# Expert stages: who releases GpSimd's scatters, and how far ahead the sync engine loads rows

## The reference

```python
x = x + attention_block(layernorm(x))   # 16 heads, learned relative bias, MLP
x = x + ffn(layernorm(x))               # 8 experts, the best 2 for each row
x = x + recurrence(layernorm(x))        # gated scan along the sequence
x = x + ffn(layernorm(x))               # the same experts once more
```

```python
probs = softmax(xf @ router_w.T)           # keep the top 2, renormalise
g = einsum('nd,edf->nef', xf, gate_w) + gate_b
u = einsum('nd,edf->nef', xf, up_w) + up_b
h = silu(g) * u
expert_out = einsum('nef,efd->ned', h, down_w) + down_b
y = einsum('ne,ned->nd', probs, expert_out)
```

## Time and profile before

| | before |
|---|---|
| time, median of 3 runs | 1426.32 us |
| lowest and highest | 1423.66, 1427.49 us |
| span of the profiled execution | 1524.2 us |
| PE, DVE, ACT, POOL busy | 80%, 75%, 63%, 65% |
| POOL's scatters (L1842), both stages | 272, 263.8 us busy |

### The profile page before, as it was taken

The page is one execution under the profiler, slowest core; times in us unless marked ns, Lnnn a source line. Parts: engine busy times, 40 slices in busy tenths (PEclk is TensorE's granted clock), DMA queues, the critical chain, the costliest instruction groups (busy, mean ns, idle before and its releaser), DMA issues. The chain is left out here.

```text
span 1524.2 us, 38116 instructions
## 1 busy us (share of the span) xinstructions
PE 1216.6 (80%) x11689; PEld 1017.3 (67%) x11689; DVE 1144.1 (75%) x3833; ACT 967.7 (63%) x2078; POOL 991.9 (65%) x1131
## 2 busy tenths in 40 slices
PE   5889999999999999973788888577787449888850
PEld 3667777777777777753788888455566348788850
DVE  5489999999999999965566665488888546666638
ACT  3588888888888888851555544277777435455420
POOL 4346688888888888777355665237777835666530
PEclk9699999999999999995799997588878669999955
DMA  7211111111111111123222222112222122222228
GB/s 199 86 46 46 48 60 60 60 60 60 59 60 60 60 60 60 39 93 83 73 86 86 81 85 68 49 49 83 73 83 69 45 68 84 86 84 84 77 83 277
DMA packets 99443, 117.19 MB, mean 77 GB/s; under 512 B 17784, under 2 KB 79792, under 8 KB 99248
## 3 DMA queue, kind: packets, MB, share of 16 engines
q1 hardware_dynamic: 70560, 73.57, 16.3%
q0 software_dynamic: 16896, 35.16, 6.8%
q10 hardware_dynamic: 11792, 6.05, 1.4%
HBM read 47.56 MB, written 41.51 MB: 58 GB/s over the span
## 5 line engine op out<-in xcount | busy, mean ns | idle before, releaser
L1153 DVE TENSOR_TENSOR ebuf<-score_banks,region 128x768 f32<-128x768 f32 x256 | 243.6, 951 | 18.8 <-PE score_banks L862 13.1
L1402 ACT ACTIVATE region<-ebuf 128x768 f32<-128x768 f32 x256 | 215.9, 860 | 23.0 <-DVE ebuf L1153 23.0
L1380 ACT CAST copied<-max_banks 128x768 bf16<-128x768 f32 x251 | 201.9, 804 | 15.1 <-PE max_banks L850 12.5
L1842 POOL DMA_INDIRECT choice_rows<-second_yo,second_xg x136 | 133.1, 979 | 112.7 <-PE second_by L1880 69.3
L1842 POOL DMA_INDIRECT choice_rows<-first_yo,first_xg x136 | 130.7, 961 | 114.0 <-PE first_by L1880 65.9
L1694 POOL DMA_INDIRECT expert_rows<-d_rows,a_d_index x112 | 129.4, 1155 | 27.9 <-issue 17.2
L1918 ACT ACTIVATE second_silu<-second_bgu,second_biases 128x256 f32<-128x256 f32 (+1 forms) x144 | 61.0, 466 | 114.3 <-PE second_bgu L1871 66.7
L1918 ACT ACTIVATE first_silu<-first_bgu,first_biases 128x256 f32<-128x256 f32 (+1 forms) x144 | 61.9, 462 | 111.8 <-issue 83.6
L1954 DVE SCALAR_TENSOR_TENSOR second_hT<-second_bgu,second_biases,second_silu 128x256 f32<-128x256 f32 (+1 forms) x144 | 62.1, 464 | 70.3 <-ACT second_silu L1918 37.6
L905 PE MATMUL bankO<-region,vaug 128*32 128x256 f32 (+1 forms) x2048 | 111.1, 334 | 1.9 <-ACT region L1402 1.9
L853 PE MATMUL max_banks<-region_r 32*128 32x256 f32 x502 | 98.3, 388 | 11.9 <-DVE ebuf L1153 7.4
(11 more groups left out here) (369 smaller groups left out, 4531.6 us busy)
## 6 DMA issues: line engine op xcount, KB each, us to landing
region_r<-region_r SPq DMA_DIRECT2D x192, 128.0 KB
first_xg<-expert_rows SPq DMA_DIRECT2D x64, 132.0 KB
second_xg<-expert_rows SPq DMA_DIRECT2D x64, 132.0 KB
z_rows<-choice_rows SPq DMA_DIRECT2D x32, 256.0 KB
c_rows<-choice_rows SPq DMA_DIRECT2D x16, 512.0 KB
out<-xres ACTq DMA_DIRECT2D x16, 256.0 KB
choice_rows<-first_yo,first_xg POOLq DMA_INDIRECT x136
choice_rows<-second_yo,second_xg POOLq DMA_INDIRECT x136
```

The source lines that it names most:

```text
L1153: nc.vector.tensor_tensor(ebuf[:, half_of_ebuf(c, j), :, :], score_banks[:, :, 0:BK], bias32[:, plain(j), :], ALU.add).then_inc(scores_fre ...
L1380: nc.scalar.copy(copied[:, 2 * j:2 * j + 2, :], banks_of_max(c, j)[:, :, 0:BK]).then_inc(maxed_free, 1)
L1402: nc.scalar.activation(p32[:, j % 4, :, :], ebuf[:, half_of_ebuf(c, j), :, :], ACT.Exp).then_inc(exped, 1)
L1842: pool.indirect_dma_start(choice_dram, bass.IndirectOffsetOnAxis(ap=xg[:, i % G, t, E:E + 1].bitcast(I32), axis=0), yo[:, i % 4, t, :], No ...
```

## The change

Both expert stages come from the same function, so both change. GpSimd no longer waits for `y_full` and `y_done`, but for one new semaphore, `rows_go`. SyncE raises it: for each turn it waits for VectorE's sum (`y_done`), raises `rows_go` by one, and then loads the rows six turns ahead. It loads six turns before the loop, where it loaded up to eight turns ahead before. The wait for `xT_full` is dropped, the one for `stored` stays. Buffers and arithmetic are the same.

```diff
-    G = 8
+    G, AHEAD = 8, 6
...
+        ..., b_ready, wh_ready, wl_ready, rows_go = (
...
                 for i in range(ST):
-                    pool.wait_ge(y_full, min(i + 2, ST))
-                    pool.wait_ge(y_done, i + 1)
+                    pool.wait_ge(rows_go, i + 1)
                     for t in range(T(i)):
                         pool.indirect_dma_start(
...
             def _(sp):
-                for i in range(ST):
-
+                def load(i):
                     if i >= G:
-                        sp.wait_ge(xT_full, i - G + 1)
                         sp.wait_ge(stored[i % 4], stored_to(i - G))
                     first = sp.value_load(...)
                     sp.dma_start(xg[:, i % G, ...], slots_dram[...]).then_inc(arrived[i % G], 16)
+
+                for i in range(AHEAD):
+                    load(i)
+                for i in range(ST):
+                    sp.wait_ge(y_done, i + 1)
+                    sp.sem_inc(rows_go, 1)
+                    if i + AHEAD < ST:
+                        load(i + AHEAD)
                 for q in range(4):
                     sp.wait_ge(stored[q], stored_to(max(range(q, ST, 4))))
```

More of the change, by code:

```diff
@@ L1820, in run_dispatched @@
         stored = [sem(f"rows_stored{i}") for i in range(4)]
-        xT_full, hi_done, lo_done, gu_full, silu_done, hid_done, y_full, y_done, b_ready, wh_ready, wl_ready = (
+        xT_full, hi_done, lo_done, gu_full, silu_done, hid_done, y_full, y_done, b_ready, wh_ready, wl_ready, rows_go = (
             sem("xT_full"), sem("hi_done"), sem("lo_done"), sem("gu_full"), sem("silu_done"), sem("hid_done"),
-            sem("y_full"), sem("y_done"), sem("biases_ready"), sem("upper_weights_ready"), sem("lower_weights_ready"))
+            sem("y_full"), sem("y_done"), sem("biases_ready"), sem("upper_weights_ready"), sem("lower_weights_ready"), sem("rows_go"))
         def stored_to(i):
```

## The result

| | before | changed |
|---|---|---|
| time, median | 1425.08 us (5 runs) | 1414.97 us (5 runs) |
| lowest and highest | 1423.64, 1427.49 us | 1411.92, 1420.54 us |
| ratio, with its 95% interval | | 0.9919 [0.9893, 0.9945] |
| PE, DVE, ACT, POOL busy | 80%, 75%, 63%, 65% (the execution of the earlier trace rows) | 82%, 81%, 70%, 70% |

The changed kernel is 0.81% faster by the ratio, some 11.5 us of 1425 (1 - 0.9919); the two medians differ by 10.1 us. The median of 1414.97 is outside the forecast's own range of 1422 to 1428 and 0.6 us from rival A's 1415.6.

A forecast was written before the change was run, and what follows sets the result against it. At 2.54 us a turn PE was taken to bound the expert stages, POOL's 2.52 close behind. Only the stage ends counted, -1.4 us from a median of 1426.3, giving 1424.9 us (own range 1422 to 1428, whole range 1413 to 1437).

The forecast's parts named there:

- rival A: Row buffers did bind PE in timed runs; earlier scatters free them: -10.7 us, 1415.6 us, chance 0.25.
- The pace in whole turns: Expert stages: profile stays at 3.2 us a turn; timed runs estimated at PE's 2.54 us.
- The ring of eight buffers: Load of turn i + 8 waits for scatter i: needs 19.0 to 21.5 of 20.3 us; gain 0, bounds 0 to 19.
- How far a scatter moves: Scatter waits for its sum, not the next down product: starts one turn earlier, 2.5 to 3.2 us.
- The end of a stage: Last two scatters of each stage: scatter 71 starts 0.7 us earlier, -1.4 us in two stages.
- The hand-over: Sum's end to scatter through SP: 0.4 us, 0.1 of it SP; bounds 0.15 and 1.5; costs nothing in whole turns.
- The loads six turns ahead: Load i waits for sum i - 6: 5.1 us left for 3.4 needed; cost 0, up to 2 us a stage.
- rival C: Loads, each hanging on a sum six turns back, come late and stall PE: 14 us, 1439 us, chance 0.10.
- Rival B: Scatters meet DVE's weight copies of `wlo` and POOL becomes the bound: +10 on the forecast, 1434.9 us, chance 0.15.
- Rival D: POOL is never idle in timed runs, so scatters start where they did, tail gains nothing: 1426.3 us, chance 0.08.

The follow-up runs named there:

- e5: Kernel before with twelve row buffers instead of eight, scatters still as late as before; 1416.06 us, ratio 0.993.
- e1: Kernel before, unedited, profiled once more; 1429.09 us, ratio 1.0013.
- e11: Kernel before, unedited, profiled another time; 1429.84 us.
- e3: Kernel before, with POOL's wait for the next down product dropped only in the last eight turns of a stage; 1424.55 us, ratio 0.9987.
- e7: Changed kernel without the relay: POOL waits for the sum itself, SP still paces its loads by it; 1414.79 us, ratio 0.9915.
- e2: Kernel before, with POOL's scatters waiting for the sum alone, SP and its loads as before; 1416.0 us, ratio 0.9929.
- e10: Changed kernel with loads five turns ahead, not six; 1475.32 us, ratio 1.0343.
- e8: Changed kernel with loads seven turns ahead, not six; 1463.42 us, ratio 1.0258.
- e6: Kernel before, with eight added one-tile buffers for the last eight loads, which then wait for no scatter; 1416.99 us, ratio 0.9939.
- e4: Changed kernel, with SP also waiting for the next down product before it releases the scatter; 1432.43 us, ratio 1.0043.
- e9: Kernel before with twelve row buffers and scatters that wait for the sum alone, no relay; 1414.35 us, ratio 0.9921.

## Why the prediction was right in part and wrong in its likeliest case

The stated range of 1413 to 1437 us holds the measured 1414.97, but the case called likeliest, 1424.9 and no measurable change, was not what happened. Rival A, the ring of buffers, did happen, with the right sum for a partly wrong reason.

- **The pace in whole turns: right in the estimate, wrong as a forecast of the profile.** The estimate that the timed runs go at PE's 2.54 us held (2.54 to 2.57 in all profiles of before and after). "The pace of 3.2 us in whole turns should stay" was wrong: 3.2 was a property of that one execution. Why it ran so is open; none of the later ones did.
- **The ring of eight buffers: the step that failed.** The prediction set the way round the ring, 19.0 to 21.5 us, against 20.3, eight whole turns, and said "I take a gain of 0". The measured way round was 20.9 us, inside those bounds, with a landing that was late; with the usual one it is about 19. What it was set against was wrong where it matters: the last loads serve one-tile turns, and eight turns from 62 on last 17.9 us (e5). With 17.9 on the other side of the comparison all of 19.0 to 21.5 is late, by 1.1 to 3.6 us; e1 showed 2.33, e11 2.05. Only the whole turns had been looked at. For the whole turns the step was nearly right: 0.8 us less in the first stage, 0.3 more in the second.
- **How far a scatter moves: over-sized.** "One turn earlier, 2.5 to 3.2 us" was 0.8 us in whole turns. The sum ends 1.0 us after its own product, so the next product is only 1.5 us away, and POOL itself had no room for more than 0.8. At turn 62 it was 1.5 us, of which 0.7 are the held scatter of turn 56, which no term of the prediction had.
- **What follows from a stall was missing.** The bound priced a wait at its own length. In the second stage the stall of 2.3 us was followed by 4.2 us of slower matmuls at the lower clock, twice what the wait cost. This term stood nowhere in the sum.
- **The end of a stage: right.** 0.7 us was expected, 0.8 measured in both stages; e3, which has this and little else, is 0.13% faster than before, a difference within its interval.
- **The hand-over: over-sized, without effect.** 0.4 us from the sum to the scatter was taken, 0.31 measured, of which SP is 0.03 (e7) and not 0.1. It lies inside the bounds of 0.15 and 1.5.
- **The loads six turns ahead: right at 0.** e7 and e2 agree within their intervals, and PE does not wait for rows in the whole turns of the changed kernel (745 to 890 us), so rival C did not happen. The estimate of 1.7 us of room fits: one turn less, 2.54 us, does not fit into it and is 3.4% slower (e10). One turn more is 2.6% slower, by the wait for landings (e8).
- **Rival B: seen, too small.** Scatters of over 1.0 us were 17 and 12 of 136 in the changed kernel, 3 and 3 in e1, and each of these 35 overlaps a copy of `wlo` on DVE, while the longest scatter of the changed kernel that overlaps none took 0.969 us. So the earlier scatters do meet the copies more often. But the median is 0.959 us in the changed kernel and 0.961 and 0.962 in e1, and the pace of PE did not change. The rule from "SBUF — State Buffer", section "SBUF: two separate sides" of the Trainium skill, by which the loser blocks for the whole instruction, would make many scatters 0.43 us longer. The trace does not agree: 97 scatters of the changed kernel have a whole copy of `wlo` within their time, at a median of 0.959 us, and the longest of all was 1.167 us.
- **Rival A's price was right by luck.** It took two thirds of the 14 us that PE had waited before transposes all along the stages in the unusual execution. The measured gain has the same size but sits in the last eight turns, mostly of the second stage.
- **Rival D** is excluded by the ratio's interval. But its ground was half right: POOL had no room for more than 0.8 us of the 1.5 that the change set free.
- **A reading that was off, without effect.** The prediction says that POOL waits 0.9 to 1.0 us of each turn of 3.19 us. 3.19 - 2.52 is 0.67; the 0.94 to 1.02 us of idle time in the earlier trace rows contain the 0.30 us that follow every scatter. No term of the sum hangs on it.

**Late landings.** From the end of a pair's second scatter to the moment when SP's wait for it is over it is mostly 1.3 to 2.2 us. For turn 62 of the second stage it was 3.44 us in e1, 3.35 in e11 and 3.49 in e3, so this late landing came back in three executions and is no accident of one. The traces' DMA packets show a companion: a packet of 16 KB in the queue that the profile's page calls instruction (q8), in e1 from 1362.48 to 1363.56 us. Of the 32 packets of turn 62's second scatter 31 had begun by 1362.5; the last one began at 1363.54. In the profiles of e1, e2, e3, e6, e7 and e11 42 of the 48 landings over 2.4 us, and all 16 over 3.0, had such a packet in flight, of the other 665 only 130. That these packets delay the scatters is argued from this, no run moved them. In e3 one ran from 1351.90 to 1353.56 us, while the rows of turn 69 were on their way. With e1's usual landing the way round the ring would have been about 19 us, still over 17.9, so the late one makes the stall longer but, by this estimate, does not make it alone. Without the 0.7 us of the held scatter as well it would be about 18, and the ring would just close.

**The clock.** That PE's stall came just before the drop is shown in e1 (2.33 us) and e11 (2.05), and in e3, where waits of 1.75 and 0.53 us came before it. e5 and e6 changed only the buffers and had neither stall nor drop, nor had e2 and the changed kernel. But no length of wait can be read from this: in e3's first stage PE waited 0.96 us at 903.4 us and the clock stayed at 1.00, and in e4's second stage it fell after a wait of 0.76 us (at 1363.3 us).

What one typical timed run gains in the last parts is not shown directly, as the two profiled executions of before (timed at 1432.9 and 1429.8 us) lie above their jobs' medians of 1425.8 and 1427.9, and those of the changed kernel (1411.9 and 1412.9) below its 1415.0. That most timed runs have the drop is likely: their granted clock over the whole run is 0.915 to 0.917 on average for the kernel before in the three jobs, 0.9145 in e3, and 0.921 to 0.924 in the changed kernel, e2, e5, e6, e7 and e9.

## What to carry to other kernels

Compare a ring of buffers with the time of the turns it really spans, the shortest ones at the end of a loop included, not with the steady pace. A consumer that is as fast as the producer in the steady pace falls behind when turns shorten, and then each needless wait ahead of it counts. A ring that just closes has no room for a landing that is 1 to 2 us late. Price a stall of PE with the slower clock that can follow it, and ask for more than one profiled execution when its span is far from the timed median.

## What the hardware showed unexpectedly

- One execution of the same program had a span of 1524.2 us where two others had 1431.1 and 1428.1, with its whole turns at 3.2 us, not 2.55.
- A pause of 2.33 us of PE (2.32 us busy in 4.6) was followed by the granted clock at half, and twelve gate and up products of a one-tile turn took 2.7 to 2.8 us, not 1.53.
- A semaphore passed on by SP cost 0.03 us more than the direct wait (0.31 and 0.28 us from the sum's end to the scatter's start).
- The landing of a scatter varied from 1.3 to 3.8 us after the end of its last scatter instruction (3.8 in the execution of the earlier trace rows), and the late ones nearly all had a 16 KB packet of the instruction queue in flight.
- The second scatter of turn 56 started 1.0 to 1.1 us after the first had ended, not 0.30, in both stages of five profiles (e1, e3, e5, e6, e11), and in none of those of the changed kernel.
